# Decoder layer on one core: value products four at a time, later base tiles in another order, causal weights zeroed on GpSimd

## The reference

```python
x = _layernorm(x + attn(x, Wqkv_w, Wqkv_b, out_w, out_b))     # 16 heads of 16, one shared key and value head, causal
x = _layernorm(x + xattn(x, ctx_512, ctx_512))                # 32 query heads of 8, 8 key/value heads, not masked
x = _layernorm(x + ffn(x, gate_w, base_gate_up, base_down, expert_gate_up, expert_down))

def xattn(q, k, v):
    scores = jnp.einsum('bkgsd,bktd->bkgst', qh, kh) / sqrt(8)
    return einsum('bkgst,bktd->bkgsd', softmax(scores), vh)

def ffn(x, ...):   # a base MLP of inner width 512, and the two best of 8 experts for each token
    base_y = silu_mul(x @ base_gate_up) @ base_down
    for e in range(8): out = out + comb[:, e:e+1] * (silu_mul(x @ expert_gate_up[e]) @ expert_down[e])
    return out + base_y
```

## Time and profile before

| | us |
|---|---|
| median of 3 runs | 708.4 (706.02, 711.39, 708.4) |
| the profiled execution: its time | 704.1 |
| its span in the trace | 701.9 |
| attention stage in the span | 0 to 391 |
| expert stage | 391 to 701.9 |
| PE busy in the span | 627.2 (89%) |
| DVE busy | 458.5 (65%) |
| ACT busy | 333.9 (48%) |
| POOL busy | 142.7 (20%) |

### The profile page before, as it was taken

One profiled execution on the slowest core, in us unless ns is written; L12 is line 12 of the kernel. 1 busy time (PEld: TensorE's weight loads), 2 busy tenths in 40 slices (PEclk: granted clock), 3 DMA queues, 4 the chain that ended last, 5 costly groups with the idle time before them and its releaser, 6 DMA issues. The chain is left out here.

```text
span 701.9 us, 11383 instructions
## 1 busy us (share of the span) xinstructions
PE 627.2 (89%) x3351; PEld 425.6 (61%) x3379; DVE 458.5 (65%) x1020; ACT 333.9 (48%) x705; POOL 142.7 (20%) x159
## 2 busy tenths in 40 slices
PE   2767999999999999999887798999999999999981
PEld 2444455555455555555433576888888788887770
DVE  3479889888988888988764583344343344344296
ACT  2355777777777777776744311132322232223114
POOL 2033110111110111110100002143433343341000
PEclk9889999999999999999968799999999999999996
DMA  8104443324443234443320681016436653110703
GB/s 263 36 1 158 157 158 128 105 102 163 166 166 131 82 119 165 165 159 121 135 98 14 230 331 31 16 53 214 170 120 223 224 165 108 47 52 19 239 1 120
DMA packets 54440, 90.47 MB, mean 129 GB/s; under 512 B 6284, under 2 KB 25231, under 8 KB 54384
## 3 DMA queue, kind: packets, MB, share of 16 engines
q1 hardware_dynamic: 50640, 80.43, 33.2%
q0 software_dynamic: 3744, 9.31, 4.2%
HBM read 56.18 MB, written 34.47 MB: 129 GB/s over the span
## 5 line engine op out<-in xcount | busy, mean ns | idle before, releaser
L1169 ACT ACTIVATE silu<-inner 128x512 f32<-128x512 f32 x55 | 32.9, 598 | 159.7 <-PE inner L1550 110.6
L486 ACT ACTIVATE prob<-scores 128x1024 f32<-128x1024 f32 x96 | 98.4, 1027 | 13.0 <-PE scores L859 8.6
L1329 DVE TENSOR_TENSOR hT<-hiddenT,hT 128x512 fp32r<-128x512 f32 x39 | 27.0, 692 | 87.9 <-ACT hT L1175 87.9
L632 DVE TENSOR_REDUCE max_c<-scores 128x8 f32<-128x1024 f32 x64 | 78.0, 1218 | 8.8 <-PE scores L922 7.2
L1545 PE MATMUL inner<-weights,sT_hi 128*128 x156 | 68.7, 440 | 0.3
L946 PE MATMUL sums<-prob,v_c 128*32 128x512 f32 x256 | 66.9, 648 | 0.0
L1135 POOL DMA_INDIRECT chosen_y<-lane_hot,to_row x39 | 40.0, 1026 | 132.2 <-DVE lane_hot L1344 132.2
L1546 PE MATMUL inner<-weights,sT_hi 128*128 x156 | 61.5, 394 | 0.0
L398 POOL TENSOR_TENSOR xT_lo<-xT_in,xT_hi 128x256 fp32r<-128x256 f32 x16 | 11.9, 745 | 236.1 <-ACT xT_hi L457 236.1
L1129 POOL DMA_INDIRECT rows<-x,from_row x39 | 38.2, 979 | 87.8 <-DVE from_row L1311 76.2
L932 PE MATMUL scores<-q_c,k_c 128*128 128x512 f32 x128 | 46.5, 445 | 5.9 <-ACT prob L486 2.8
(11 more groups left out here) (218 smaller groups left out, 1430.0 us busy)
## 6 DMA issues: line engine op xcount, KB each, us to landing
split_w<-halves SPq DMA_DIRECT2D x32, 768.0 KB, 5.3
weights<-split_w SPq DMA_DIRECT2D x8, 3072.0 KB, 12.8
raw_w<-in_expert_w SPq DMA_DIRECT2D x16, 768.0 KB, 4.6
weights<-chosen_y SPq DMA_DIRECT2D x8, 512.0 KB, 7.5
xT_in<-in_xT SPq DMA_DIRECT2D x16, 128.0 KB, 4.6
x_in<-in_x SPq DMA_DIRECT2D x16, 128.0 KB, 3.6
x<-stream SPq DMA_DIRECT2D x16, 128.0 KB, 4.6
ctxT_in<-in_ctxT SPq DMA_DIRECT2D x16, 96.0 KB, 4.0
```

The costliest lines, as they stand in the source:

```text
L486: act.activation(prob[:, m, :], scores[:, n, :], ACT.Exp, scale=scale).then_inc(sem[exped], 1)
L632: dve.tensor_reduce(out_[:, 8 * unit:8 * unit + 8], scores[:, n, :].rearrange("p (h k) -> p h k", k=S), AX.X, ALU.max).then_inc(sem[read], 1)
```

## The change

- `s_sum`: units 0 and 1 become one. Four products with 32 columns of values each, one at each quarter of the array's columns, in one group. `c_sum`: the four units become two, each of four products of 32 columns; the second unit adds to the same PSUM places as the first (its values lie 16 columns further on in `v_c`, the rest are zeros), so both halves of the cross-attention end in one bank.
- So one `s_read`, one `c_read`, four transposes and one reciprocal remain for each attention in a step, where there were two copies, eight transposes and two reciprocals. The two multiplications of each remain.
- The mask products of `s_main` go. In their place POOL runs `s_causal` on each unit of `prob` after its exponential: an `affine_select` in place over 128x1024 values that keeps a weight where the query's index is not below the key's, and writes zero elsewhere. `s_sum` waits for it.
- `prob`'s slots come free later: both self-attention slots when the one `s_sum` is done, the cross-attention's in pairs.
- The lists are changed to suit: `c_sum` 0 moves from the end of a step to behind `s_res` of the next, `s_sum` stands once, behind `s_qkv`, where unit 1 stood; `s_read` behind `w_high` 1; POOL's list gets `s_causal` 0 first and `s_causal` 1 behind `c_keys`.
- Expert stage: `HT_RING` 8 for 5. PE makes all chunks of the last two base groups and then both groups' output tiles; DVE's order at the end follows.

```diff
-HT_RING = 5
+HT_RING = 8
 PE_ORDER = [
     ("s_proj", 0, 1), ("c_max", 2, 0), ("s_main", 0, 2), ("s_turn", 0, 3), ("c_max", 3, 0), ("s_res", 0, 1),
-    ("c_sum", 1, -1), ("s_main", 1, 2), ("c_shift", 0, 0), ("c_sum", 2, -1), ("s_max", 0, 3), ("c_sum", 3, -1),
-    ("c_main", 0, 0), ("c_out", 0, -1), ("s_sum", 0, 2), ("c_main", 1, 0), ("c_out", 1, -1), ("s_max", 1, 3),
-    ("c_turn", 0, 1), ("c_main", 2, 0), ("s_out", 0, 2), ("c_max", 0, 1), ("s_qkv", 0, 4), ("s_sum", 1, 2),
-    ("s_shift", 0, 3), ("c_main", 3, 0), ("s_out", 1, 2), ("c_max", 1, 1), ("c_sum", 0, 0),
+    ("c_sum", 0, -1), ("s_main", 1, 2), ("c_shift", 0, 0), ("s_max", 0, 3), ("c_sum", 1, -1),
+    ("c_main", 0, 0), ("c_main", 1, 0), ("c_out", 0, -1), ("s_max", 1, 3),
+    ("c_turn", 0, 1), ("c_main", 2, 0), ("c_max", 0, 1), ("s_qkv", 0, 4), ("s_sum", 0, 2),
+    ("s_shift", 0, 3), ("c_main", 3, 0), ("s_out", 0, 2), ("c_max", 1, 1),
     ("x2_logit", 0, -3), ("x2_turn", 0, -2),
 ]
 ACT_ORDER = [
...
-    ("s_split", 0, 4), ("c_read", 0, -1), ("c_rsqrt", 0, -2), ("s_exp", 1, 2), ("s_log", 0, 1),
-    ("s_rsqrt", 0, 1), ("w_high", 0, 2), ("c_read", 1, -1), ("c_rows", 0, 1), ("c_exp", 0, 0), ("s_read", 0, 2),
-    ("c_exp", 1, 0), ("c_turn", 0, 1), ("c_exp", 2, 0), ("c_values", 0, 1), ("w_high", 1, 2), ("s_read", 1, 2),
+    ("s_split", 0, 4), ("c_rsqrt", 0, -2), ("s_exp", 1, 2), ("s_log", 0, 1),
+    ("s_rsqrt", 0, 1), ("w_high", 0, 2), ("c_read", 0, -1), ("c_rows", 0, 1), ("c_exp", 0, 0),
+    ("c_exp", 1, 0), ("c_turn", 0, 1), ("c_exp", 2, 0), ("c_values", 0, 1), ("w_high", 1, 2), ("s_read", 0, 2),
     ("c_exp", 3, 0), ("s_rows", 0, 4), ("x2_logit", 0, -3), ("x2_read", 0, -2),
 ]
 DVE_ORDER = [
-    ("s_den", 1, 1), ("s_out", 1, 1), ("c_max", 1, 0), ("s_rows", 0, 3), ("s_proj", 0, 1),
+    ("s_den", 0, 1), ("s_out", 0, 1), ("c_max", 1, 0), ("s_rows", 0, 3), ("s_proj", 0, 1),
...
-    ("c_ln", 0, -2), ("w_low", 0, 1), ("c_rows", 0, 1), ("w_low", 1, 1), ("c_den", 0, -1), ("c_den", 1, -1), ("c_out", 0, -1), ("c_out", 1, -1),
-    ("s_max", 1, 3), ("c_res", 0, -1), ("s_den", 0, 2), ("c_stats", 0, -1), ("s_out", 0, 2), ("c_max", 0, 1), ("s_bias", 0, 4), ("w_low", 2, 1),
+    ("c_ln", 0, -2), ("w_low", 0, 1), ("c_rows", 0, 1), ("w_low", 1, 1), ("c_den", 0, -1), ("c_out", 0, -1),
+    ("s_max", 1, 3), ("c_res", 0, -1), ("c_stats", 0, -1), ("c_max", 0, 1), ("s_bias", 0, 4), ("w_low", 2, 1),
     ("s_shift", 0, 3),
 POOL_ORDER = [
-    ("s_split", 0, 4), ("c_keys", 0, 1), ("x_bias", 0, 2), ("base_split", 0, 2),
+    ("s_causal", 0, 2), ("s_split", 0, 4), ("c_keys", 0, 1), ("s_causal", 1, 2), ("x_bias", 0, 2), ("base_split", 0, 2),
...
-PROB_USE = {"s_exp": ("s_summed", 2), "c_exp": ("c_summed", 4)}
+PROB_USE = {"s_exp": ("s_summed", 1), "c_exp": ("c_summed", 2)}
...
+            def s_causal(seq, b):
+                m = prob_ring.slot("s_exp", b, seq)
+                wait(pool, sem["s_exp"], seq, 2, b + 1)
+                keys_first = prob[:, m, :].rearrange("p (h q) -> p h q", q=S)
+                pool.affine_select(keys_first, keys_first, [[0, 8], [1, S]], ALU.is_ge, no_weight, base=0, channel_multiplier=-1)\
+                    .then_inc(sem["s_causal"], 1)
...
                 for bank in range(2):
                     at = 512 * bank
-                    pe.matmul(scores[:, n, at:at + 512], ident_b[:], mask_kq[:], start=True, stop=False)
...
-            def s_sum(seq, b):
+            def s_sum(seq, unit):
+                p, n = seq.odd, sum_ring.slot("s_sum", 0, seq)
+                wait(pe, sem["s_causal"], seq, 2)
...
                 for h in range(2):
-                    mm = pe.matmul(sums[64 * h:64 * h + 64, n, :], v_s[p][:], prob[:, m, 512 * h:512 * h + 512], start=True, stop=True)
+                    for b in range(2):
+                        at = 64 * h + 32 * b
+                        mm = pe.matmul(sums[at:at + 32, n, :], v_s[p][:], prob[:, prob_ring.slot("s_exp", b, seq), 512 * h:512 * h + 512],
+                                       start=True, stop=True)
...
+            def c_sum(seq, a):
+                p, n = seq.odd, sum_ring.slot("c_sum", 0, seq)
+                wait(pe, sem["c_exp"], seq, 4, 2 * a + 2)
...
+                for j in range(4):
+                    m, v = prob_ring.slot("c_exp", 2 * a + j // 2, seq), j % 2
+                    mm = pe.matmul(sums[32 * j:32 * j + 32, n, :], v_c[p][:, P * a + 32 * j:P * a + 32 * j + 32],
+                                   prob[:, m, 512 * v:512 * v + 512], start=(a == 0), stop=(a == 1))
...
-            for m in range(CHUNKS):
+            for m in range(CHUNKS - 1):
                 multiply(u + m)
             first = FIRST_OUTS + SORTED
-            later = [[0, 1], [2, 3], [4, 5], [6, 7]]
-            for m in range(TILES):
+            next_up = u + CHUNKS - 1
+            multiply(next_up)
+            add_shares(0)
+            multiply(next_up + 1)
+            for t in (1, 2):
+                add_shares(t)
+            multiply(next_up + 2)
+            for t in (3, 4):
+                add_shares(t)
+            multiply(next_up + 3)
+            add_shares(5)
+            for m in range(2 * TILES):
                 take(first + m)
...
+                if m == 2 * TILES - 2:
+                    variance(0)
+                    newton(0)
+                if m < 2 * TILES - 1:
+                    add_shares(6 + m)
...
-            base_chunk(GROUPS_FIRST + 1, 0)
+            for c in range(CHUNKS):
+                base_chunk(GROUPS_FIRST + 1, c)
             base_outer(GROUPS_FIRST)
-            for c in range(1, CHUNKS):
-                base_chunk(GROUPS_FIRST + 1, c)
             base_outer(GROUPS_FIRST + 1)
```

More of the change, by code:

```diff
@@ L101 @@
     "s_shift": [("s_shift_read", 1, 1)],
-    "s_out": [("s_ctx", 2, None)],
+    "s_out": [("s_ctx", 1, 1)],
     "s_proj": [("s_ctx_read", 1, 1)],
@@ L178, in rings @@
             name, per = PROB_USE[stage]
-            prob.append((stage, unit, 0, delta, name, per, unit + 1))
+            prob.append((stage, unit, 0, delta, name, per, unit // 2 + 1))
     for stage, unit, delta in PE_ORDER:
@@ L183, in rings @@
             score.append((stage, unit, 0, delta, name, per, unit + 1))
-        if stage == "s_sum" or stage == "c_sum" and unit % 2 == 0:
+        if stage in SUM_USE and unit == 0:
             name, per = SUM_USE[stage]
-            summed.append((stage, unit, 0, delta, name, per, (unit if stage == "s_sum" else unit // 2) + 1))
+            summed.append((stage, unit, 0, delta, name, per, 1))
         for part, (name, per, upto) in enumerate(MISC_USE.get(stage, [])):
@@ L432, in c_keys @@
                 ins.then_inc(sem["ctx_k_set"], 1)
[L434 removed]
+            run(pool, POOL_ORDER, dict(s_causal=s_causal, s_split=s_split, x_bias=bias, c_keys=c_keys, base_split=split_base))
         @block.scalar
@@ L447, in c_values @@
                 wait_loaded(act, ctx_loaded, seq, 2)
-                wait(act, sem["c_summed"], seq.back(2), 4)
-                act.copy(v_c[p][:].rearrange("p a (j s) -> p a j s", j=4)[:, :, :, 0:XD],
+                wait(act, sem["c_summed"], seq.back(2), 2)
+                act.copy(value_places(v_c[p])[:, :, :, 0:XD],
                          ctx_in[p][:].rearrange("p (a j d) -> p a j d", a=2, j=4)).then_inc(sem["ctx_v_set"], 1)
@@ L466, in s_rows @@
                 wait(act, sem["s_k_full"], seq.back(1))
-                wait(act, sem["s_summed"], seq.back(2), 2)
+                wait(act, sem["s_summed"], seq.back(2))
                 q = qkv[:, 0:D].rearrange("p (n c) -> p n c", c=32)
@@ L494, in s_read @@
             def s_read(seq, unit):
-                n = sum_ring.slot("s_sum", unit, seq)
-                wait(act, sem["s_summed"], seq, 2, unit + 1)
-                wait(act, sem["s_out_full"], seq.back(1), 2, unit + 1)
-                act.copy(sumT_s[:, unit, :], sums[:, n, :]).then_inc(sem["s_sum_read"], 1)
+                n = sum_ring.slot("s_sum", 0, seq)
+                wait(act, sem["s_summed"], seq)
+                wait(act, sem["s_out_full"], seq.back(1))
+                act.copy(sumT_s[:], sums[:, n, :]).then_inc(sem["s_sum_read"], 1)
             def c_read(seq, a):
-                n = sum_ring.slot("c_sum", 2 * a, seq)
-                wait(act, sem["c_summed"], seq, 4, 2 * a + 2)
-                wait(act, sem["c_out_full"], seq.back(1), 2, a + 1)
-                act.copy(sumT_c[:, a, :], sums[:, n, :]).then_inc(sem["c_sum_read"], 1)
+                n = sum_ring.slot("c_sum", 0, seq)
+                wait(act, sem["c_summed"], seq, 2)
+                wait(act, sem["c_out_full"], seq.back(1))
+                act.copy(sumT_c[:], sums[:, n, :]).then_inc(sem["c_sum_read"], 1)
             def s_proj(seq, unit):
@@ L934, in c_main @@
                 mm.then_inc(sem["c_main_full"], 1)
-            def c_sum(seq, unit):
-                p, a, m = seq.odd, unit // 2, prob_ring.slot("c_exp", unit, seq)
-                n = sum_ring.slot("c_sum", 2 * a, seq)
```

(16 more changed lines are left out.)

120 lines of the change are left out of this document (54 added, 66 removed).

## The result

The changed kernel takes 752.4 us (median of 4 runs, 751.0 to 770.0); the kernel before, run beside it, 707.2 (705.6 to 711.4). The ratio is 1.064, interval 1.057 to 1.070: slower by 45 us, where 5 us less were forecast, and outside the range of 684 to 718.

What follows compares the result with a forecast made beforehand. PE bounds the kernel before; after the change a chain of slot waits holds steps at 21.4 us. Terms +1.6 +1.8 +0.4 -1 -4 -5.3 +1.5 = -5.0 take the median from 708.4 to 703.4, said as 703; range 684 to 718.

Steps and rivals of the forecast that it cites:

- rival A: Full attention steps: a closed chain of waits for `prob`'s slots holds them at 21.4 us for 21.2; total 703, chance 0.5.
- second link: Part of the chain in a full step: DVE from s_newton to `s_max` 1, put at 4.8 us.
- So up to 3.5 each is hidden: POOL's two selections per attention step: up to 3.5 us each fits in ten microseconds before `s_sum`; 2 us each assumed.
- The first step with both kinds of scores, "0": First attention step with both kinds of scores (19.49 us): no `c_sum`, so wait (1) is absent; change 0.
- Wait (2): Attention step: `c_exp` 2 waits for `s_exp` 0's `prob` slot until `s_sum` is done; ACT idle about 2 us per step.
- wait (1): Attention step: `s_exp` 0 waits for the last step's `c_exp` 0 slot until `c_sum` 0 is done; DVE idle 0.8 before `c_shift`.
- +1.5 taken: Clock term of the sum: PE gets idle spells of 1 to 1.7 us in each step; +1.5 us in all.
- rival C: Full steps: PE busy three quarters, clock low a quarter of the time; 1.6 us a step, 721 us, chance 0.2.
- Emptying: Attention from 312 us on: no `s_sum`, fewer products, copies and transposes; -4 us (bounds -1 and -8).
- the filling: Four steps that fill the pipeline: fewer products beside long waits; -1 us (bounds 0 and -3).
- the end: Expert stage's end: DVE's last share 4 us earlier, ACT's 12 rows no longer delay the second logarithm; -5.3 us.
- Rival B: Full steps: DVE sets the pace at 19.45 us, total 679; middle case 693; chance 0.2 for both together.

Runs made afterwards that it cites:

- Waits alone: Changed kernel with GpSimd's `c_keys` ahead of the first selection and 16 unused bf16 products per step on PE; 716.3 us, ratio 1.013 to the kernel before.
- the masks back: Changed kernel with the causal mask made by bf16 mask products again and no selections on POOL; 748.5 us, ratio 1.063 to the kernel before.
- all three edits: Changed kernel with `c_sum` 0 at a step's end, `s_sum` between `c_main` 0 and 1, `c_keys` first on POOL; 686.3 us, ratio 0.973 to the kernel before.
- The end alone: Kernel before with only the expert stage's end changed (HT_RING 8, new order of PE and DVE); 699.4 us for 703.9, ratio 0.993.
- both sums moved: Changed kernel with `c_sum` 0 at a step's end and `s_sum` between `c_main` 0 and 1, POOL's list unchanged; 699.7 us, ratio 0.989 to the kernel before.

## Why the prediction was wrong, point by point

**Where 50 us went.** In ratios of 707 us: the change has +6.4%, without the falls of the clock +3.2%, with `c_keys` first besides +1.3%. So the clock costs some 22 us, the hold by `k_c` some 13, and 9 remain, where -5 was forecast. The shares depend on the order: with `c_keys` first alone the kernel has +5.7%, so that the hold is worth some 5 us, not clear of the noise, and the clock some 31. The clock is the largest in both. Of the 14 us between 9 and -5 most is in the eleven steps: with both edits they take 248.5 us for 230.2, and 3 more were forecast. Of the other 15, 6.3 lie in the first step and 9 in the ten after it.

**The chain of waits (rival A): right in mechanism, its second link mis-sized.** In the step of the change at 275 to 299 the links are 7.26, 6.68, 6.71 and 3.29, forecast as 7.0, 4.8, 6.4 and 3.3 (the second's own terms give 4.73, and with it the sum is 21.4), read off the rows above (`max_c` 292.34 to s_newton 299.60; s_newton of the step before, 275.66, to `max_s` 282.34; to s_out's transposes at 289.05; to 292.34). With the clock full and `k_c` out of the way, 7.26, 5.33, 6.41 and 3.29, sum 22.29. The step that failed is the one that took DVE's stretch "189.02 to 194.79, less idle and one reciprocal" over from the trace of before: it took each instruction's duration with it, while the change put two POOL instructions beside them. The two holds are 0.86 and 0.73 us in each step. Of the 0.6 that the second link still has too much with `k_c` out of the way, 0.45 is again a hold, L749's beside the selection most of all. Why the first link is 0.3 longer than its rows isn't shown.

**"So up to 3.5 each is hidden": right for s_sum, wrong as a price.** The selection takes 1.09 us for the 2 assumed, and POOL is idle most of the step. But POOL's list was costed at nothing beyond its own length. Moving `k_c` some 2 us later against s_newton (from 2.43 ahead of it to 0.53), behind a selection that waits for s_exp 0, was a step of the change that the prediction did not follow. What became late was not POOL's work but DVE's beside it. The Trainium skill, page SBUF — State Buffer, section Who interferes with whom, says that VectorE and GpSimd share one pair of ports as an exclusive lock, kept for the whole instruction by whoever issues first, and that a VectorE instruction with two SBUF inputs contends with a GpSimd one that reads SBUF. The trace agrees: L737 has two inputs in SBUF and ends with POOL's instruction, while L731 and L734, with one tensor and a scalar for each partition, take 0.21 on the same 128x1 tiles beside the same `k_c`. The section also names `tensor_scalar` in a faster two-port mode; L749 is a `tensor_scalar` of 128x256 and was held, but no trace shows in which mode it ran.

**The first step with both kinds of scores, "0": wrong by 6.** Wait (2) is in it, and wait (1) falls into the end of the same stretch, where s_exp 0 of the next step stands. In the change itself the step takes 26.25 at a clock of 0.87, with L737 and L749 at 1.18 and 0.79, only 0.7 more than before; with the masks back it takes 24.85 without any new hold. So here the waits and the fallen clock are most of it. The holds of 2.01 and 2.52, with `base_split` beside them, are for the run "Waits alone".

**The clock, "+1.5 taken": wrong; rival C happened as well.** C gave 1.6 us a step and 721. Its mechanism is in the trace, a clock of 0.69 to 0.93 in every full step, and its price is 22 to 31 us, where C gave 19 and the sum took 1.5. This is the term that was mis-sized most. The failed step is treating C as an alternative to A, with a chance of 0.2, where it is a consequence of it: in A's own step PE is busy three quarters and stands 2.8, 1.1 and 1.3 us (forecast: spells of 1 to 1.7). The evidence set against it, a step with PE busy 85% and the clock at 1.00, was true (the kernel with all edits has such steps) and did not bear on A. A small slip besides: with the level low a sixth of the time, C's own numbers give 714, 0.9% slower and not over 1%.

**Emptying, the filling and the end.** For the filling -1 was forecast: the first of the eleven steps begins at 62.9 for 61.7, and at 63.9 in "The end alone", whose attention is that of before, so -1 can't be read here. From the last of the eleven steps to the first `base_hT` it is 107.3 before (clock 0.87), 121.2 in the change (0.70), 107.3 with the unused products (0.90) and 102.0 with `c_keys` first besides (0.93). So the forecast -4 came, as -5.3, only with clock and hold out of the way. The end gave 5.3 in the trace and 4.6 in the run by itself, of 5.3 forecast; DVE's last shares and PE's tiles follow each other as written, with one wait of PE of 1.87 that was not foreseen. The forecast's terms for DVE's last share add to 4.45, were said as 4, and it came 3.9 earlier; a DVE idle spell of 0.71 that no term had is in it, so that this number is right in part by luck.

**Rival B.** Its step of 19.45 was right for a kernel without the chain, which the change is not. Its two terms were not: DVE's 18.3 and gaps of 1.15 were forecast, 18.85 and 0.6 measured, so the match of the sum is luck. Its sign, DVE busy over 93% of a step, did not show in the change (84%); it does in the kernel with all three edits (97%).

**What stays open.** Why the clock falls in one full step and not in the next of the same kernel isn't settled by these runs; they only show that filling the idle spells removes it. Nor is it separated how much of the first step's 6.3 us in "Waits alone" is waiting and how much its holds; both at once need not add up. With waits and no new hold it takes 24.85 (masks back), with holds of 2.31 and 2.52 and neither wait 24.25 (both sums moved), each with a fallen clock.

## What to carry to other kernels

When an instruction moves on an engine with a low load, look for what runs beside its new place, not only for who waits for it: here one of DVE's smallest instructions became as long as the POOL instruction beside it, and the trace of before had a row of the kind. When a ring's reader is moved later to save work, count uses against slots first; one line of more slots, or the reader's old place, was worth 50 us here. And where a forecast says that TensorE will wait in each step, the clock is a term of that same forecast, not a separate case.

## What the runs showed of the hardware

- A DVE instruction with two inputs of 128x1 values took 0.16 us alone, 1.02 beside `k_c`, and 2.01 beside `x_bias` and a cast of 128x1024: it ended when POOL's did. Those with one such input and a scalar for each partition kept their 0.21 beside the same `k_c`. A normalisation of 128x256 went from 0.41 to 1.14 beside the selection, and to 2.52 beside `base_lo`.
- An `affine_select` over 128x1024 fp32 values took 1.09 us, near the cast of that size (1.03) and not the subtraction of 2.39.
- 16 unused bf16 products per step brought the granted clock of ten of the eleven steps to 1.00 and made the kernel 22 us faster.
- Four value products, one at each quarter of the columns, took 1.06 us.
